# Output pass of a two-layer graph network: x loaded ahead, added to in place and stored from where it stands

## What is computed

```python
def L0(h, ...):                       # first layer
    gate = silu(edge_attr @ W1.T + b1) @ W2.T + b2 + adapt_logit
    msg  = gate * h[dst] * (cw * mj)[:, None]
    agg  = segment_sum(msg, src) / clip(segment_sum(mj, src), 1e-8)[:, None]
    return layernorm(h + agg) * gamma + beta

def L1(h, ...):                       # second layer, 8 relations
    h1  = relu(einsum('ni,rij->nrj', h, weight1) + bias1)
    h2  = einsum('nrj,rjo->nro', h1, weight2)
    agg = segment_sum(h2[src, rel_type] * norm, dst)
    return relu(agg + bias2)

h = relu(layernorm(x)); x = x + L0(h, ...)
h = relu(layernorm(x)); x = x + L1(h, ...)
return x
```

## Time and profile before

| | |
|---|---|
| median of three runs | 1534.34 us (1529.28 to 1535.26) |
| the profiled execution | 1533.91 us |
| its span, first to last instruction | 1532.2 us |
| busy: DVE, PE, POOL, ACT | 87%, 76%, 67%, 40% of the span |
| DMA, all queues | 268.72 MB, 175 GB/s on average |

### The profile page before, as it was taken

The page is one execution under the profiler, slowest core; times in us unless marked ns, Lnnn a source line. Parts: engine busy times, 40 slices in busy tenths (PEclk is TensorE's granted clock), DMA queues, the critical chain, the costliest instruction groups (busy, mean ns, idle before and its releaser), DMA issues.

```text
span 1532.2 us, 20105 instructions
## 1 busy us (share of the span) xinstructions
PE 1157.1 (76%) x5198; PEld 846.7 (55%) x5198; DVE 1336.7 (87%) x3937; ACT 618.2 (40%) x1423; POOL 1025.5 (67%) x809
## 2 busy tenths in 40 slices
PE   5898999989999989991047878888888888886000
PEld 2677777777777777771035555555555555554000
DVE  6999999999999999880299999999999999993598
ACT  2544444544445444440034444444444444442000
POOL 7655567777887676666537887887878878866100
PEclk9756555655556565555556565555655655557555
DMA  7999986666666566642446665555555555533899
GB/s 228 305 320 333 325 228 155 153 145 145 142 164 154 136 155 138 147 103 11 130 156 169 170 161 139 140 139 140 138 137 139 140 141 139 140 71 58 295 396 390
DMA packets 154389, 268.72 MB, mean 175 GB/s; under 512 B 73818, under 2 KB 90411, under 8 KB 153380
## 3 DMA queue, kind: packets, MB, share of 16 engines
q1 hardware_dynamic: 78228, 223.53, 43.5%
q0 software_dynamic: 68992, 24.64, 17.5%
q10 hardware_dynamic: 7056, 19.27, 3.1%
HBM read 194.33 MB, written 112.55 MB: 200 GB/s over the span
## 4 chain that ended last, share of the span: by engine, by line
PE 32%; DMA 20%; DVE 19%; POOL 15%; issue 11%; ACT 3%; SPq 1%; POOLq 0%; ACTq 0%; DVEq 0%
POOL agg L468 11%; PE ps_m L555 11%; DMA t<-agg,src_all 6%; PE ps_m L644 6%; PE ps_qs L555 4%; DMA agg<-x,once 3%; PE ps_k L630 3%; DMA lows<-low 2%; DVE x L1038 2%; DVE same L834 2%; DMA agg<-y,once 2%; DVE t L1042 2%; POOL nodes L426 2%; DMA agg<-ysq,once 2%; POOL agg L504 2%
## 5 line engine op out<-in xcount | busy, mean ns | idle before, releaser
L504 POOL DMA_INDIRECT agg<-sums,once x196 | 317.8, 1621 | 89.5 <-issue 64.1
L426 POOL DMA_INDIRECT nodes<-in_table,dst_all x196 | 194.1, 990 | 104.0 <-issue 50.2
L495 POOL DMA_INDIRECT t<-agg,src_all x196 | 190.3, 971 | 83.7 <-issue 49.1
L555 PEld LDWEIGHTS ps_m<-msg,same 128*128 128x128 f32 x980 | 200.4, 314 | 29.8 <-issue 29.8
L555 PE MATMUL ps_m<-msg,same 128*128 128x48 f32 x980 | 208.2, 398 | 1.0 <-issue 1.0
L630 PE MATMUL ps_k<-h_t,rw_sb 56*128 56x256 f32 x588 | 132.3, 571 | 96.3 <-ACT hid L724 73.7
L555 PEld LDWEIGHTS ps_qs<-msg,same 128*128 128x128 f32 x980 | 183.0, 288 | 2.1 <-DVE msg L926 2.1
L555 PE MATMUL ps_qs<-msg,same 128*128 128x49 f32 x980 | 180.1, 362 | 2.0 <-DVE msg L926 2.0
L468 POOL DMA_INDIRECT agg<-x,once x84 | 135.1, 1609 | 49.0 <-issue 21.9
L630 PEld LDWEIGHTS ps_k<-h_t,rw_sb 56*128 56x128 f32 x588 | 67.6, 260 | 144.6 <-ACT hid L724 100.6
L644 PE MATMUL ps_m<-hid,rw_sb 128*64 128x256 f32 x588 | 136.1, 634 | 0.0
(11 more groups left out here) (149 smaller groups left out, 2575.1 us busy)
## 6 DMA issues: line engine op xcount, KB each, us to landing
agg<-in_both SPq DMA_DIRECT2D x14, 2758.0 KB
t<-agg SPq DMA_DIRECT2D x49, 784.0 KB, 4.4
kept<-kept_out SPq DMA_DIRECT2D x49, 404.0 KB, 2.8
kept_in<-kept SPq DMA_DIRECT2D x49, 404.0 KB
agg<-bias_rows SPq DMA_DIRECT2D x49, 384.0 KB
out<-t ACTq DMA_DIRECT2D x49, 384.0 KB, 5.8
rows<-in_src_rows SPq DMA_DIRECT2D x49, 256.0 KB, 4.1
rows<-in_dst_rows SPq DMA_DIRECT2D x49, 256.0 KB, 3.2
```

What stands on the lines that cost most here:

```text
L426: pool.indirect_dma_start(nodes[s][:, t, :], None, table, bass.IndirectOffsetOnAxis(ap=dst_all[:, c:c + 1], axis=0)).then_inc(nodes_in[b % ...
L495: pool.indirect_dma_start(t2[b % T2S][:, t, :], None, wide, bass.IndirectOffsetOnAxis(ap=src_all[:, c:c + 1], axis=0)).then_inc(ends_in[b ...
L504: pool.indirect_dma_start(agg1, bass.IndirectOffsetOnAxis(ap=once1[b % LAG1][:, t:t + 1], axis=0), sums1[b % LAG1][:, t, :], None, compute ...
L555: last = mm(ps[:, t * width:(t + 1) * width], kept_same[:, at:at + P], m[:, v, :], start=(v == t), stop=(v == TILES - 1))
```

## The change

`agg_last` has six slots instead of four; two more of them lie in `x2`. `x_last` has a buffer for each of the 11 chunks of `x_mid` (six in `t2`, three in `kept_in`, two in `same`), and SP loads all of them before it waits for POOL's adds; ahead of the tenth it waits for the last sums, because `same` is read until then. The chunks are taken in another order: the 38 resident ones first, then the 11. Beta is added in place, at first to 24 chunks (`BETA`) before the loop, and within the loop 24 chunks ahead. The max-and-add writes into x itself, and ACT stores from there, so that `out_sb`, `x_beta` and the wait for a stored slot go. At the end SP waits for one semaphore.

```diff
-SLOTS = 4
+SLOTS = 6
+BETA = 24
...
-        agg_last = [y[:, 0:NR, :].rearrange("p r h -> p (r h)"), ysq[:, 0:NR, :].rearrange("p r h -> p (r h)"),
-                    halves[:, 0:PC], halves[:, PC:2 * PC]]
-        x_last = [w[:, 0:PC] for w in (kept_in[0], kept_in[1], kept_in[2], t2[2][:, :, :].rearrange("p r w -> p (r w)"))]
+        def flat(w):
+            return w[:, :, :].rearrange("p r h -> p (r h)")
+
+        agg_last = [flat(w)[:, 0:PC] for w in (y, ysq, x2[0], x2[1])] + [halves[:, 0:PC], halves[:, PC:2 * PC]]
+        x_last = ([flat(w)[:, k * PC:(k + 1) * PC] for w in t2 for k in range(2)] + [w[:, 0:PC] for w in kept_in]
+                  + [w[:, 0:PC] for w in same])
+        last_order = list(range(NBLOCK - RES, NBLOCK)) + list(range(NBLOCK - RES))
+
+        def x_final(b):
+            return x_last[b] if b < NBLOCK - RES else flat(x_rows(b)[:, TILES:G, :])
...
-            for b in range(SLOTS):
-                load_mid(b)
+            for b in range(NBLOCK - RES):
+                if b >= 2 * T2S + T2S:
+                    sp.wait_ge(S["sums1_done"], NBLOCK)
+                sp.dma_start(x_last[b], x_mid[b]).then_inc(S["mid_in"], 16)
             sp.wait_ge(S["added1"], 16 * COLS)
-            for b in range(NBLOCK):
-                s = b % SLOTS
-                need(sp, S["out_done"], b - SLOTS + 1)
-                sp.dma_start(agg_last[s][:, :], agg1_chunks[b]).then_inc(last_in[s], 16)
-                if b >= SLOTS:
-                    load_mid(b)
-            for s in range(SLOTS):
-                sp.wait_ge(out_stored[s], 16 * ((NBLOCK - 1 - s) // SLOTS + 1))
+            for k, b in enumerate(last_order):
+                s = k % SLOTS
+                need(sp, S["out_done"], k - SLOTS + 1)
+                sp.dma_start(agg_last[s], agg1_chunks[b]).then_inc(last_in[s], 16)
+            sp.wait_ge(S["out_stored"], 16 * NBLOCK)
...
-            for b in range(NBLOCK):
-                s = b % SLOTS
-                act.wait_ge(S["out_done"], b + 1)
-                act.dma_start(out_chunks[b], out_sb[s][:, :]).then_inc(out_stored[s], 16)
+            for k, b in enumerate(last_order):
+                act.wait_ge(S["out_done"], k + 1)
+                act.dma_start(out_chunks[b], x_final(b)).then_inc(S["out_stored"], 16)
...
-            for b in range(NBLOCK):
-                s = b % SLOTS
-                stored = (NBLOCK - RES - 1 - s) // SLOTS + 1
-                dve.wait_ge(last_in[s], 16 * uses(b, SLOTS) + 16 * min(uses(b, SLOTS), stored))
-                mid = x_last[s][:, :].rearrange("p (r h) -> p r h", r=NR) if b < NBLOCK - RES else x_rows(b)[:, TILES:G, :]
-                V.tensor_tensor(x_beta[b % 2][:, :, :], mid, each(beta_b[:, :], NR),
-                                ALU.add).then_inc(S["x_beta_done"], 1)
-                dve.wait_ge(S["x_beta_done"], b + 1)
-                need(dve, out_stored[s], 16 * (b // SLOTS))
-                V.scalar_tensor_tensor(out=out_sb[s][:, :], in0=agg_last[s][:, :], scalar=0.0,
-                                       in1=x_beta[b % 2][:, :, :].rearrange("p r h -> p (r h)"),
+            def add_beta(b):
+                rows = x_final(b).rearrange("p (r h) -> p r h", h=H)
+                V.tensor_tensor(rows, rows, each(beta_b[:, :], NR), ALU.add).then_inc(S["x_beta_done"], 1)
+
+            for b in last_order[0:BETA]:
+                add_beta(b)
+            for k, b in enumerate(last_order):
+                if k + BETA < NBLOCK:
+                    if last_order[k + BETA] == 0:
+                        dve.wait_ge(S["mid_in"], 16 * (NBLOCK - RES))
+                    add_beta(last_order[k + BETA])
+                dve.wait_ge(last_in[k % SLOTS], 16 * uses(k, SLOTS))
+                dve.wait_ge(S["x_beta_done"], k + 1)
+                V.scalar_tensor_tensor(out=x_final(b), in0=agg_last[k % SLOTS], scalar=0.0, in1=x_final(b),
                                        op0=ALU.max, op1=ALU.add).then_inc(S["out_done"], 1)
```

More of the change, by code:

```diff
@@ L223, in build @@
         halves = hid1[:, :, :, :].rearrange("p k h n -> p (k h n)")
-        agg_last = [y[:, 0:NR, :].rearrange("p r h -> p (r h)"), ysq[:, 0:NR, :].rearrange("p r h -> p (r h)"),
-                    halves[:, 0:PC], halves[:, PC:2 * PC]]
-        x_last = [w[:, 0:PC] for w in (kept_in[0], kept_in[1], kept_in[2], t2[2][:, :, :].rearrange("p r w -> p (r w)"))]
+        def flat(w):
[3 more added lines that the diff above has]
+                  + [w[:, 0:PC] for w in same])
+        assert len(agg_last) == SLOTS and len(x_last) >= NBLOCK - RES
+        last_order = list(range(NBLOCK - RES, NBLOCK)) + list(range(NBLOCK - RES))
+        def x_final(b):
+            return x_last[b] if b < NBLOCK - RES else flat(x_rows(b)[:, TILES:G, :])
         sums_in = ([(w[:, :, :].rearrange("p r h -> p (r h)"), 4) for w in (y, ysq, x2[0], x2[1])]
@@ L230, in build @@
                 for w, fit in sums_in for k in range(fit)][0:LAG]
-        x_beta = [v[:, 0:NR, :] for v in x2]
-        out_sb = [t2[k // 2][:, :, :].rearrange("p r w -> p (r w)")[:, k % 2 * PC:(k % 2 + 1) * PC] for k in range(SLOTS)]
         def psum(name, shape):
@@ L263, in build @@
         last_in = ring_of(sem, SLOTS, "last_in")
-        out_stored = ring_of(sem, SLOTS, "out_stored")
         names = ("idx_in consts_in types_in_done src_in_done rw1_in rb1_in wide_set agg1_set low_stored added0 added1 "
@@ L276, in build @@
                  "m1t_done msg1_done same1_done turned1_done once1_done sums1_done sums1_copied "
-                 "x_beta_done out_done").split()
+                 "x_beta_done out_done mid_in out_stored").split()
         S = {n: sem(n) for n in names}
@@ L392, in _ @@
                 sp.wait_ge(x_stored[p], 16 * ((NBLOCK - RES - 1 - p) // 2 + 1))
-            def load_mid(b):
-                if b < NBLOCK - RES:
-                    sp.dma_start(x_last[b % SLOTS][:, :], x_mid[b]).then_inc(last_in[b % SLOTS], 16)
-            for b in range(SLOTS):
-                load_mid(b)
-            sp.wait_ge(S["added1"], 16 * COLS)
-            for b in range(NBLOCK):
-                s = b % SLOTS
-                need(sp, S["out_done"], b - SLOTS + 1)
-                sp.dma_start(agg_last[s][:, :], agg1_chunks[b]).then_inc(last_in[s], 16)
-                if b >= SLOTS:
-                    load_mid(b)
-            for s in range(SLOTS):
-                sp.wait_ge(out_stored[s], 16 * ((NBLOCK - 1 - s) // SLOTS + 1))
+            for b in range(NBLOCK - RES):
+                if b >= 2 * T2S + T2S:
+                    sp.wait_ge(S["sums1_done"], NBLOCK)
+                sp.dma_start(x_last[b], x_mid[b]).then_inc(S["mid_in"], 16)
+            sp.wait_ge(S["added1"], 16 * COLS)
+            for k, b in enumerate(last_order):
[3 more added lines that the diff above has]
+            sp.wait_ge(S["out_stored"], 16 * NBLOCK)
         @blk.gpsimd
```

## The result

The changed kernel is slower: 1542.79 us against 1535.04 (medians of ten runs each), ratio 1.0047 with a 95% interval of 1.0031 to 1.0063. Its profiled execution took 1542.97 us, 9.06 more than that of the kernel before; the span is 1541.2. I forecast 1530.5 and a range of 1525 to 1536.5.

What follows compares the result with a forecast made beforehand. Transfers were taken to bound the output pass, with DVE close behind, and POOL's chain alone the drain. From the profiled 1533.91 us, -6.7 - 2.4 + 0.8 + 4.9 = -3.4 gave 1530.5 us, range 1525 to 1536.5.

Steps and rivals of the forecast that it cites:

- The pass: Output pass, from the first load of the sums to the end: to shrink from 107.4 to 98.3 us.
- Its bytes: Output pass: seven x_mid loads leave it, 2.75 MB at 410 GB/s, 6.7 us less.
- The other 2.4 us: Output pass: six slots and no output slot remove the early hole (1.5) and the dip (0.9); bounds 0 and 2.9.
- the depth of the slots: Start of the output pass: six loads instead of four keep DMA supplied until slots return, 1.5 us less.
- DVE lies just off the path: Output pass: a DVE pair takes 1.88 us, one load and one store 1.92 us; costed at nothing.
- The landing: Drain: nine early x_mid loads delay one block's scatter-add landing, +0.8 us; bounds nothing or 2.5 us.
- The train: Drain: 25 beta adds beside POOL's scatter-adds, 2.64 us a step instead of 1.85, +4.9 us; bounds 0 and 7.
- rival 3: Drain: a train without a gap never lets POOL in, +19.3 less 9.1 gained, 1544.1 us; chance 0.04.
- Rival 1: Drain: the beta adds do not hold POOL, 1525.6 us; chance 0.27 together with the rival that the change fails.

Runs made afterwards that it cites:

- p1: The changed kernel with beta copied once to PSUM and read from there by all adds of beta; 1527.12 us, ratio 0.9958 to the kernel before.
- e6: The changed kernel with `BETA = 1` and its x_mid loads spread (three, four, four); 1520.20 us, ratio 0.9938 to the kernel before.
- e7: e6 with four slots for the sums instead of six; drain 31.8 us, pass 97.9 us.
- e10: The changed kernel with `BETA = 1` and four early x_mid loads, the other seven issued in the pass; drain 31.5 us, pass 104.7 us.
- p4: The changed kernel with a tiny single-operand reduction after each of the first 24 adds of beta; 1519.57 us in a single run.
- e5: The kernel before with 25 back-to-back two-SBUF-operand DVE instructions added ahead of the output pass's wait, no load moved; 1540.89 us.
- e8: The changed kernel with its x_mid loads spread (three, four, four) and the train of adds kept; 1531.90 us.
- m2: Kernel without a layer: scatter-adds sent straight behind a semaphore wait into two-SBUF-operand DVE trains of 16; 63 of 64 took 1.54 to 2.35 us.
- m1: Kernel without a layer: scatter-adds sent behind a memset into DVE trains of 16; all 28 beside two-SBUF-operand trains took 1.55 to 2.34 us.
- m3: Kernel without a layer: scatter-adds meeting two-SBUF-operand DVE trains of 24 at varied depth and phase; 1.71 to 2.20 us at 2.5 to 3.9 instructions in.

## Why the prediction was wrong

*The pass* was right: 97.5 us, forecast 98.3. Its bytes cost what was said. The other 2.4 us were of the right size (3.2 came) for partly wrong reasons: the depth of the slots, on which I put 1.5, makes at most 0.4. That DVE lies just off the path held: a pair takes 1.74 us now, where its add lies 24 chunks ahead of its max-and-add, against 1.90 us for a load and a store (0.787 MB at 415 GB/s).

*The landing* was mis-sized: +0.8 forecast, +3.6 measured (+4.3 in p1), outside my bound of 2.5. The row with four loads (3.43 against 3.21) was no guide. The two times count from the start of POOL's instruction, and that one took 1.85 us instead of 1.54, which is all of the difference: the four loads cost the landing nothing. They were over when the instruction ended at 1394.90: from 1394 to 1396 all queues together moved 12 GB/s. In the changed kernel it ended at 1395.07, and from 1394 to 1398 still 364 to 366 GB/s moved. e6, e7 and e10, with three or four loads early, have the short landing back, and p1 to p4, with nine, keep the long one; so it is the number of loads in flight at that moment.

*The train* is the step that failed: "I therefore take 2.64 us a step in place of 1.85". That an add with both operands in SBUF holds POOL was right, and e5 and e8 show the step itself, 2.60 us; in the changed kernel it never came. What failed is the assumption that POOL waits for no more than the add then running (0.44 us for the first of a block, and the next turn of the train for each that follows). This holds only while POOL asks within about four adds (3.5 us) of the train's start or of the last time that it was let in. A block's landing takes 3.96 us from start to start, 4.6 adds, which was too long in e5 and e8 and in one of m2's twenty trials, and the first request of all, put off by the loads, came 7.3 adds into the train. I had priced this as rival 3 at 0.04 and named as its condition "POOL is held for eight successive adds or more"; it came to 17.7. The argument against it rested on the comparison of 1185, which stood third in its row, too early to show the hold. Rival 3's time was 1544.1; the profiled run took 1542.97, as the first load of the pass moved by 18.9 us instead of 19.3 and the pass gained 0.8 more. Rival 1 (no stall) does not hold: a scatter-add took 16.90 us beside TENSOR_TENSOR with both operands in SBUF, and those of e5 and e8 that were let in took 1.79 to 2.30, against 1.54 with one operand in PSUM. The Trainium skill, SBUF — State Buffer, section "Who interferes with whom", reports a probe in which tensor_tensor did not stall a DMA; these runs do not agree. The Trainium skill's rule in the same section that the later one is blocked until the first is done agrees with the sawtooth of m2, and goes too short for a train: there it is all of them, not the one then running.

*The sum*: -6.7 - 2.4 + 0.8 + 4.9 = -3.4 was forecast; -9.9 + 3.6 + 15.1 = +8.8 came, and with 0.1 of later start this is, but for rounding, the 9.0 of the spans.

## What to carry to other kernels

Idle time of an engine is not free room: before work is hoisted into it, ask what runs beside it and what both of them read. Beside indirect DMAs from POOL, keep VectorE from running more than three instructions of this size in a row with both operands in SBUF. One operand in PSUM took the cost away here, and so did a reduction of 8 elements between the instructions (one execution). And look first whether the hoisted work was on the path at all: here `BETA = 1` does the same for the pass and costs nothing.

When loads are brought forward, spread them so that few are in flight when a small transfer that gates the chain has to land.

## What the runs showed of the hardware

- A scatter-add of POOL beside a dense train of DVE instructions with two SBUF operands (0.869 us each) waits for the rest of the one then running (1.54 to 2.35 us) in all 57 trials of m1, m2 and m3 that asked up to 4.1 instructions into the train. In m3 all 33 that asked 4.2 to 14.8 instructions in were held until the train ended plus 1.42 us, 18.72 us at the longest. Passed all the same: m2's first, at 4.9, and 19 of m2's 20 that asked 4.2 to 4.7 instructions after a scatter-add let in.
- The same train with one operand in PSUM leaves it at 1.54 us (p1, with never more than 4.4 adds between two requests). A reduction of 0.15 us between the two-operand instructions let it in at 4.8 instructions (p4, 1.59 us). A multiplication by a constant, one operand in SBUF, adds 0.13 to 0.20 us (m1, 3.8 to 4.4 instructions in only).
- Loads and stores of 384 KB together hold 415 GB/s for 80 us (changed kernel, 1457 to 1537). Nine such loads issued within 5 us lengthen the landing of a 128-row scatter-add by 3.6 us in the changed kernel and 4.3 in p1. Four, which were over when it ended, leave it as it is (before, e10).
